# KV sums copied by ScalarE, norms rounded by GpSimd, and projected halves taken ahead of features

## The chip, the cores and the metric

The kernel runs on one core of a Trainium2 chip. The metric is the device time in microseconds of one execution. The engines are named as the profile names them: PE (TensorE), ACT (ScalarE), DVE (VectorE), POOL (GpSimd) and SP (SyncE, which here issues most of the DMAs). Each engine works through its own instruction queue in order, and waits on semaphores for the others.

## The reference

A batch of 8 sequences, 1024 tokens of 512 channels each, float32, goes through linear attention with random features, a layer norm, a matmul with a ternary weight, and a second layer norm. Cut to what matters:

```python
def feature_map(x, orf):                       # 16 heads of 32 channels, 128 features
    proj = x @ orf.T / d_k ** 0.25
    norm = jnp.sum(x * x, axis=-1, keepdims=True) / (2.0 * math.sqrt(d_k))
    return (jnp.exp(proj - norm) + EPS) / math.sqrt(m)

q = feature_map(split(x @ Wq.T + bq), orf)
k = feature_map(split(x @ Wk.T + bk), orf)
v = split(x @ Wv.T + bv)
kv = jnp.einsum('nlm,nld->nmd', k, v)
ksum = jnp.sum(k, axis=1)
out = jnp.einsum('nlm,nmd->nld', q, concatenate([kv, ksum[..., None]], axis=-1))
out = (out[..., :-1] / out[..., -1:]) @ Wo.T + bo
x = layernorm(x + out)
x = layernorm(x + x @ (ternary(weight) * scale).T)
```

## The kernel before, in words

Float32 products are made of rounded parts: every operand is split into a high part (rounded by ACT) and a low part (the rest, by DVE or POOL), and a product is hi·hi + hi·lo + lo·hi.

The heads go in four groups of four (`g`), and each group is two units: an even unit `u = 2g` for the keys and an odd unit `u = 2g + 1` for the queries. A batch is units 0 to 7 and then the output stages. The order of everything is one list of stages, `SCHEDULE`, written by hand in `unit_stages` (lines 72 to 146) and `output_stages`. Every engine walks through this same list and does its own part of each stage, so a stage that is moved in the list moves in the queue of every engine that has a part in it. There is no planner with costs.

While unit `u` is at work, unit `u + 2` is projected and prepared. The stages, with `h` for a half of 512 tokens:

- `P` (line 951, PE): six of the twelve matmuls that project a half; two `P` stages make a half in one PSUM bank. The banks 0 and 1 alternate, and `P` waits for `L` of the half that had the bank before.
- `S` (lines 649 and 651, ACT): the projected half is copied to `unit_hi` and squared to `squares`. `L` (816, DVE): `unit_lo`.
- `Q` (824, 828, DVE): squares transposed and summed. `N` (834 to 839, DVE): the unit's norms are transposed (`norms_turned`), rounded (837) and the rest taken (839) into `norm_rows`.
- `LIFT` (SP): twelve DMAs bring `unit_hi` and `unit_lo` into `stacks`. `NL` (570, POOL): two DMAs bring the norm rows there.
- `F` (964 for keys, 969 for queries, PE; 668, ACT): products with the random features, then the exponential into `features`. For keys DVE adds the eight feature tiles up (777 for the first two, 780), in the same stages `F`.
- `G` (982, PE; the eight of a group): kv sums of the keys. With the last one, products of `ones` with DVE's added features (991), then ACT's copies (673, 678, 680). `KVT` (999, 1000, PE): kv sums transposed; ACT makes two small products with EPS (685, 687); DVE copies the transposed sums from PSUM into `kv_ksum` (842).
- `GG` (1014, PE): numerators and denominators of a half of the queries, which waits for `kv_ksum`; DVE transposes and inverts denominators (850, 853, 855). `R` (865, 867, DVE): the division.
- `XT` (636, ACT; 809, DVE; 580, POOL): the next batch's input split into `x_hi` and `x_lo`, in unit 5. Its first projection, at the end of unit 5, waits for `x_lo` of tile 3.
- In the output stages, `A`, `O`, `LN`, `Y`, `YT`, `FF`, `ST`, and `V` of the next batch (937 to 939). `Q` and `N` of the next batch's unit 1 stand there, too. `V`, `O` and `FF` share banks 0 and 1 with `P`.
- In the last batch (`b + 1 == B`), unit 5 has an order of its own, in which `KVT` follows `S` of half 1, and unit 7 has stages `AG` and `OK` in place of the whole-row output stages.

In batch 0, DVE also makes the ternary weights (`WF`, 755 and 756) between the stages of units 1 to 4.

Of the kernel before, what the change touches and what calls it, by code (L numbers as in the profile page):

```python
# [44 lines left out]
P = 128  # L45
# [26 lines left out]
def unit_stages(b, u):  # L72
# [24 lines left out]
    if is_key(u):  # L97
        st = [[("ST", b - 1, t)] if u == 0 and b else [] for t in (TT - 2, TT - 1)]
        half = [("G", b, g, r) for r in range(split_at(b, g))]
        early = [("AG", b, 0, 0), ("AG", b, 1, 0)] if b + 1 == B and u + 2 == NU else []  # L100
        if u == 0:
            seq = f(0, 1) + p[1] + s0 + l0 + f(2, 3) + q0 + st[0] + p[2] + f(4, 5) + half + s1 + l1 + f(6, 7) + q1 + norm + lift
            seq += st[1] + p[3]
        else:
            seq = f(0, 1) + p[0] + f(2, 3) + p[1] + s0 + l0 + f(4, 5) + q0 + half + p[2] + early + f(6, 7) + s1 + l1 + q1 + norm + lift + p[3]
        if u == 0 and b == 0:
            seq += [("WA", 0, k) for k in range(KT)]
        if u == 2 and b == 0:
            seq += [("WF", 0, 1)]
        if u == 2 and 0 < b < B - 1:  # L110
            seq += [("LX", b + 1, t) for t in range(5)]
        return seq
    kv = [("G", b, g, r) for r in range(split_at(b, g), 8)]
    if u < NU - 1:
        seq = p[0] + f(0, 1)
        if u == 1 and b == 0:
# [4 lines left out]
        elif u < NU - 3:  # L121
            seq += kv + f(2, 3) + p[1] + [("KVT", b, g)] + s0 + l0 + f(4, 5) + p[2] + f(6, 7) + s1 + q0 + [("GG", b, g, 0)]
            seq += l1 + p[3] + [("R", b, g, 0), ("GG", b, g, 1)] + q1 + norm + lift
        else:
# [121 lines left out]
def attention_kernel(nc, x, xt, wq, wk, wv, wo, wff, bias, bo, orf, out):  # L246
# [5 lines left out]
    with ctx:  # L252
# [68 lines left out]
        a_exp, a_kc = Signal("features_ready", 8 * NU), Signal("kv_copied", 3 * NG)  # L321
        a_c = Signal("eps_sums_ready", 2 * NG)
        a_ahi = Signal("a_hi_ready", TT)
        a_y, a_yhi, a_out = Signal("y_ready", TT), Signal("y_hi_ready", TT), Signal("out_ready", TT)

        v_xlo, v_plo, v_n = Signal("x_lo_ready", 4, 4), Signal("unit_lo_ready", 2 * NU), Signal("norms_ready", 3 * NU, 2)
        v_sq, v_ns = Signal("squares_read", 2 * NU, 2), Signal("squares_summed", 2 * NU, 2)
        v_ks = Signal("features_added", 7 * NG)
        v_kvc = Signal("kv_ready", NG)
        v_dt, v_dr = Signal("den_turned", 2 * NG, 1), Signal("den_steps", 2 * 2 * NG)  # L330
# [3 lines left out]

        g_xlo = Signal("x_lo_ready_pool", 4)
        g_xb = Signal("x_plus_bias_ready", TT)
        a_ghi, v_glo = Signal("group_hi_ready", 0), Signal("group_lo_ready", 0)
# [185 lines left out]
        def _(pool):  # L523
# [37 lines left out]
            def lift_norms(b, u):  # L561

                slot = ST[:, u % 2, :].bitcast(F32)
                wait(t_f.sem, t_f.nth(b, 8 * (u - 1)))
                if u == 1:
                    wait(t_ff.sem, t_ff.nth(b, 0))
                wait(v_n.sem, v_n.nth(b, 3 * u + 3))
                for part in range(2):
# [4 lines left out]
            for kind, b, at, _, _ in steps():  # L573
# [8 lines left out]
                elif kind == "A":  # L582
                    pool.wait_ge(d_xr[t].sem, d_xr[t].nth(b, 1))
                    if b + 1 == B and t < 2:
                        pool.wait_ge(v_kvc.sem, v_kvc.nth(b, NG))
                    elif b + 1 == B and t < 4:
# [10 lines left out]
        def _(act):  # L597
# [21 lines left out]
            for kind, b, at, ps, _ in steps():  # L619
# [62 lines left out]
                elif kind == "KVT":  # L682
# [3 lines left out]
                                         scale=EPS).then_inc(a_c.sem, 1)  # L686
                    nc.scalar.activation(CC[:, 2 * u:2 * u + 1], RSUM[:, 2 * u:2 * u + 1], ACT.Copy, scale=EPS).then_inc(a_c.sem, 1)
                elif kind == "A" and b + 1 < B:
                    split_hi(b, u)
# [21 lines left out]
        def _(dve):  # L711
# [76 lines left out]
            for kind, b, at, ps, _ in steps():  # L788
# [30 lines left out]
                elif kind == "Q":  # L819
# [6 lines left out]
                    if h == 0:  # L826
                        dve.wait_ge(v_n.sem, v_n.nth(b, 3 * (u - 1) + 1))
                    nc.vector.reduce_sum(NSUM[:, 16 * h:16 * (h + 1)], TQ[:, :].rearrange("p (a c) -> p a c", c=DH),
                                         axis=mybir.AxisListType.X).then_inc(v_ns.sem, 1)
                elif kind == "N":  # L830
                    n = 3 * u
                    dve.wait_ge(v_ns.sem, v_ns.nth(b, 2 * u + 2))
                    dve.wait_ge(v_n.sem, v_n.nth(b, n))
                    nc.vector.transpose(NT[:, :], NSUM).then_inc(v_n.sem, 1)
                    dve.wait_ge(v_n.sem, v_n.nth(b, n + 1))
                    norms_lifted(dve, b, u - 2)
                    nc.vector.tensor_copy(NN[:, u % 2, 0, :], NT[:, :]).then_inc(v_n.sem, 1)
                    dve.wait_ge(v_n.sem, v_n.nth(b, n + 2))
                    nc.vector.tensor_tensor(NN[:, u % 2, 1, :], NT[:, :], NN[:, u % 2, 0, :].bitcast(F32), ALU.subtract).then_inc(v_n.sem, 1)  # L839
                elif kind == "KVT":  # L840
                    dve.wait_ge(t_kvt.sem, t_kvt.nth(b, u + 1))
                    nc.vector.tensor_copy(KVS[:, u % 2, :], DN[:, 0:2 * P]).then_inc(v_kvc.sem, 1)
                elif kind == "F" and is_key(u) and not sums_on_pe(b, u // 2):
# [58 lines left out]
        def _(pe):  # L902
# [14 lines left out]
            for kind, b, at, ps, old in steps():  # L917
# [83 lines left out]
                elif kind == "GG":  # L1001
                    g, half = u, at[1]
                    if half == 0:

                        pe.wait_ge(v_kvc.sem, v_kvc.nth(b, g + 1))
                    else:
# [78 lines left out]
```

## Time and profile before

| what | value |
| --- | --- |
| median of 3 runs | 1294.76 us (1294.49 to 1295.84) |
| profiled execution, its own time | 1293.62 us |
| its span, first to last instruction | 1291.8 us |
| granted TensorE clock, mean | 0.999 |
| PE busy | 1262.5 us, 98% |
| DVE busy | 940.8 us, 73% |
| ACT busy | 700.6 us, 54% |
| POOL busy | 326.6 us, 25% |

The table's busy times are shares of the span, and an engine that isn't the bottleneck may be idle at no cost. Matmuls are pipelined: a matmul of 512 columns is shown with 0.39 us, but in an undisturbed row of them each starts 0.228 us after the one before. So a wait of PE is read best from the distance of two starts, against the same distance where nothing waits; the idle column of the trace shows somewhat less than that. Likewise ACT and DVE start an instruction some 0.1 us before the one ahead has ended.

### The profile page before, as it was taken

How to read it: one execution, taken by the hardware profiler on the slowest of the kernel's cores; microseconds unless marked ns; L12 is line 12 of the kernel's file. 1: busy time of each engine (PE TensorE's matmuls, PEld its weight loads, DVE VectorE, ACT ScalarE, POOL GpSimd, SP SyncE). 2: the span in 40 equal slices, each digit the busy share in tenths (PEclk: the TensorE clock that was granted, in tenths of full speed). 3: DMA queues.
4: the chain of work that ended last, by engine and by line, in shares of the span. 5: the costliest groups of instructions: out<-in, count | busy, mean ns of one | idle time of the engine just before them, and what ended most of it. 6: DMA issues, size and time to landing. Idle time of an engine off the chain costs nothing.

```text
span 1291.8 us, 24909 instructions
## 1 busy us (share of the span) xinstructions
PE 1262.5 (98%) x8626; PEld 958.8 (74%) x8626; DVE 940.8 (73%) x1775; ACT 700.6 (54%) x1403; POOL 326.6 (25%) x617
## 2 busy tenths in 40 slices
PE   9999999999999999999999999999999999999986
PEld 8767788677877678776787768876788767886665
DVE  6588765887658875788757886588865787657766
ACT  5557435574356743567336663367534665446534
POOL 0102342024310243103431034211252022420043
PEclk9999999999999999999999999999999999999999
DMA  6658404783146821567215762258612685036611
GB/s 236 153 125 220 100 33 121 171 195 88 52 110 174 201 61 58 129 171 187 62 58 130 181 169 65 65 132 209 153 44 71 152 208 142 33 87 144 149 58 65
DMA packets 82749, 160.33 MB, mean 124 GB/s; under 512 B 17856, under 2 KB 36416, under 8 KB 82112
## 3 DMA queue, kind: packets, MB, share of 16 engines
q1 hardware_dynamic: 68880, 139.78, 43.4%
q10 hardware_dynamic: 9648, 16.85, 3.4%
q0 software_dynamic: 4096, 2.11, 0.7%
q8 instruction: 69, 1.13, 0.4%
q14 instruction: 56, 0.46, 0.1%
HBM read 39.13 MB, written 16.78 MB: 43 GB/s over the span
## 4 chain that ended last, share of the span: by engine, by line
PE 76%; DVE 10%; issue 5%; ACT 4%; POOL 0%; ACTq 0%; DVEq 0%; POOLq 0%
PE ps L951 21%; PE ps L914 18%; PE ps L1014 7%; PE ps L964 6%; PE ps L982 5%; PE ps L937 4%; PE ps L939 4%; PE ps L938 4%; PE ps L969 4%; PE ps L1040 2%; ACT features L668 1%; DVE squares_turned L824 1%; DVE den L865 1%; DVE unit_lo L816 1%; DVE dens_turned L850 1%
## 5 line engine op out<-in xcount | busy, mean ns | idle before, releaser
L668 ACT ACTIVATE features<-ps 128x512 f32<-128x512 f32 x512 | 278.7, 604 | 248.2 <-PE ps L964 168.8
L570 POOL DMA_DIRECT2D stacks<-norm_rows x128 | 69.5, 546 | 530.4 <-DVE norm_rows L839 256.8
L964 PEld LDWEIGHTS ps<-orf_stack,stacks 98*128 98x128 f32 x1024 | 130.9, 192 | 28.0 <-issue 20.3
L914 PE MATMUL ps<-Wo_hi,stacks 128*128 128x512 f32 x448 | 150.5, 402 | 0.0
L641 ACT ACTIVATE values_then_attention<-ps 128x512 f32<-128x512 f32 x64 | 38.2, 597 | 196.9 <-PE ps L939 193.8
L780 DVE TENSOR_TENSOR den<-den,features 128x512 f32<-128x512 f32 x186 | 128.1, 689 | 12.9
L964 PE MATMUL ps<-orf_stack,stacks 98*128 98x128 f32 x1024 | 130.5, 272 | 0.0
L1014 PE MATMUL ps<-features,kv_ksum 128*32 128x512 f32 x1024 | 123.1, 598 | 3.3 <-ACT features L668 2.1
L816 DVE SCALAR_TENSOR_TENSOR unit_lo<-ps,cols,unit_hi 128x512 fp32r<-128x512 f32 x128 | 94.3, 736 | 39.0 <-ACT squares L651 39.0
L550 POOL TENSOR_SCALAR stats<-stats 128x1 f32<-128x1 f32 x128 | 36.0, 282 | 334.9 <-DVE stats L767 334.8
L914 PE MATMUL ps<-W_ternary,stacks 128*128 128x512 f32 x448 | 110.7, 389 | 0.0
L951 PE MATMUL ps<-x_hi,Wq_hi 128*128 128x512 f32 x256 | 103.5, 404 | 6.5 <-DVE unit_lo L816 6.5
L951 PE MATMUL ps<-x_hi,Wk_hi 128*128 128x512 f32 x256 | 108.5, 424 | 1.3 <-DVE x_lo L809 1.3
L937 PE MATMUL ps<-Wv_hi,x_hi 128*128 128x512 f32 x256 | 102.6, 401 | 0.8
L616 ACT ACTIVATE rows<-rows,stats 128x512 f32<-128x512 f32 x112 | 88.3, 815 | 26.4 <-POOL stats L554 25.6
L914 PEld LDWEIGHTS ps<-Wo_hi,stacks 128*128 128x128 f32 x448 | 84.2, 188 | 24.3 <-issue 7.1
L951 PE MATMUL ps<-x_lo,Wq_hi 128*128 128x512 f32 x256 | 101.1, 395 | 0.0
L951 PE MATMUL ps<-x_lo,Wk_hi 128*128 128x512 f32 x256 | 100.8, 394 | 0.0
L951 PE MATMUL ps<-x_hi,Wq_lo 128*128 128x512 f32 x256 | 100.6, 393 | 0.0
L951 PE MATMUL ps<-x_hi,Wk_lo 128*128 128x512 f32 x256 | 100.2, 391 | 0.0
L939 PE MATMUL ps<-Wv_hi,x_lo 128*128 128x512 f32 x256 | 100.0, 391 | 0.0
L938 PE MATMUL ps<-Wv_lo,x_hi 128*128 128x512 f32 x256 | 100.0, 390 | 0.0
(132 smaller groups left out, 2528.0 us busy)
## 6 DMA issues: line engine op xcount, KB each, us to landing
stacks<-unit_hi SPq DMA_DIRECT2D x512, 128.0 KB, 2.4
stacks<-unit_lo SPq DMA_DIRECT2D x256, 128.0 KB, 2.8
out<-rows ACTq DMA_DIRECT2D x56, 256.0 KB, 2.0
rows<-in_x_t SPq DMA_DIRECT2D x49, 256.0 KB, 3.4
rows<-in_x SPq DMA_DIRECT2D x32, 256.0 KB, 3.8
features<-in_x SPq DMA_DIRECT2D x32, 256.0 KB, 4.1
values_then_attention<-in_x_t SPq DMA_DIRECT2D x8, 256.0 KB, 7.4
stacks<-norm_rows POOLq DMA_DIRECT2D x128, 16.0 KB, 2.7
```

What stands on the lines that cost most here:

```text
L570: pool.dma_start(slot[row:row + 1, :].rearrange("o (t c) -> o t c", c=DH), NN[:, u % 2, part, :].bitcast(F32)).then_inc(n_lifted[u % 2].se ...
L616: nc.scalar.activation(row, row, ACT.Identity, scale=ln(k, t, 10), bias=ln(k, t, 11))\
L668: nc.scalar.activation(FE[:, n % 8, :, 0:M], ps[:, :].rearrange("p (a m) -> p a m", a=HG), ACT.Exp, scale=C_EXP).then_inc(a_exp.sem, 1)
L780: ins = nc.vector.tensor_tensor(total, total, FE[:, r, :, 0:M], ALU.add)
L816: nc.vector.scalar_tensor_tensor(out=EL[:, u % 2, half], in0=ps[:, :], scalar=BC[:, u:u + 1], in1=EH[:, u % 2, half].bitcast(F32), op0=ALU ...
L914: last = mm(out, a, b, start=(n == 0), stop=(n == len(terms) - 1))
L937: mm(ps[:, :], XH[:, k, c], WH["v"][:, k, :], start=(k == 0), stop=False)
L938: mm(ps[:, :], XH[:, k, c], WL["v"][:, k, :], start=False, stop=False)
L939: last = mm(ps[:, :], XL[:, k, c], WH["v"][:, k, :], start=False, stop=(k == KT - 1))
L951: last = mm(ps[:, :], *terms[n], start=(n == 0), stop=(n == len(terms) - 1))
L964: last = mm(ps[:, M * h:M * (h + 1)], slot[0:QK, L * h + P * r:L * h + P * (r + 1)], ORF[0:QK, h, :], start=True, stop=True)
L1014: last = mm(bank[DH * h:DH * (h + 1), :], KVS[:, g % 2, c + DH * h:c + DH * (h + 1)], FE[:, HG * half + h, :, 0:M], start=True, stop=True, ...
```

## The change

Four things:

1. The copy of the transposed kv sums (stage `KVT`) goes from DVE to ACT, behind ACT's two small products. Who waited for DVE's signal (PE in `GG`, POOL in `A` of the last batch) waits for ACT's.
2. In `N`, DVE only transposes the norms. POOL rounds them and takes the rest, at the beginning of its stage `NL`, and issues the two DMAs as before. DVE's next transposition waits for POOL's reading of the last one.
3. In even units other than 0, `S` and `L` stand right behind the `P` that ends their half, ahead of `F` (with its exponentials and additions); `Q` of half 0 stands behind the next `P`.
4. In units 1 and 3 the same: `S` and `L` of half 0 are the second thing in the unit, ahead of `F(0, 1)` and `G`; `S` and `L` of half 1 stand ahead of `F(6, 7)`; `Q` of half 0 takes their old place behind `KVT`. At the unit's end, `Q` of half 1 goes ahead of `GG` of half 1, and both divisions `R` go to the end. Units 0, 5 and 7 keep their order.

```diff
-            seq = f(0, 1) + p[0] + f(2, 3) + p[1] + s0 + l0 + f(4, 5) + q0 + half + p[2] + early + f(6, 7) + s1 + l1 + q1 + norm + lift + p[3]
+            seq = f(0, 1) + p[0] + s0 + l0 + f(2, 3) + p[1] + q0 + f(4, 5) + half + p[2] + early + s1 + l1 + f(6, 7) + q1 + norm + lift + p[3]
...
-        seq = p[0] + f(0, 1)
+        seq = p[0] + (s0 + l0 if u < NU - 3 else []) + f(0, 1)
...
-            seq += kv + f(2, 3) + p[1] + [("KVT", b, g)] + s0 + l0 + f(4, 5) + p[2] + f(6, 7) + s1 + q0 + [("GG", b, g, 0)]
-            seq += l1 + p[3] + [("R", b, g, 0), ("GG", b, g, 1)] + q1 + norm + lift
+            seq += kv + f(2, 3) + p[1] + [("KVT", b, g)] + q0 + f(4, 5) + p[2] + s1 + l1 + f(6, 7) + [("GG", b, g, 0)]
+            seq += p[3] + q1 + [("GG", b, g, 1)] + norm + lift + [("R", b, g, 0)]
...
             def lift_norms(b, u):
                 slot = ST[:, u % 2, :].bitcast(F32)
+                pool.wait_ge(v_n.sem, v_n.nth(b, u + 1))
+                norms_lifted(pool, b, u - 2)
+                nc.gpsimd.tensor_copy(NN[:, u % 2, 0, :], NT[:, :]).then_inc(g_n.sem, 1)
+                pool.wait_ge(g_n.sem, g_n.nth(b, 2 * u + 1))
+                nc.gpsimd.tensor_tensor(NN[:, u % 2, 1, :], NT[:, :], NN[:, u % 2, 0, :].bitcast(F32), ALU.subtract)\
+                    .then_inc(g_n.sem, 1)
                 wait(t_f.sem, t_f.nth(b, 8 * (u - 1)))
                 if u == 1:
                     wait(t_ff.sem, t_ff.nth(b, 0))
-                wait(v_n.sem, v_n.nth(b, 3 * u + 3))
+                wait(g_n.sem, g_n.nth(b, 2 * u + 2))
...
+                    act.wait_ge(t_kvt.sem, t_kvt.nth(b, u + 1))
+                    nc.scalar.activation(KVS[:, u % 2, :], DN[:, 0:2 * P], ACT.Copy).then_inc(a_kv.sem, 1)
...
                 elif kind == "N":
-                    n = 3 * u
                     dve.wait_ge(v_ns.sem, v_ns.nth(b, 2 * u + 2))
-                    dve.wait_ge(v_n.sem, v_n.nth(b, n))
+                    if b or u:
+                        dve.wait_ge(g_n.sem, g_n.nth(b, 2 * u))
                     nc.vector.transpose(NT[:, :], NSUM).then_inc(v_n.sem, 1)
-                    dve.wait_ge(v_n.sem, v_n.nth(b, n + 1))
-                    norms_lifted(dve, b, u - 2)
-                    nc.vector.tensor_copy(NN[:, u % 2, 0, :], NT[:, :]).then_inc(v_n.sem, 1)
-                    dve.wait_ge(v_n.sem, v_n.nth(b, n + 2))
-                    nc.vector.tensor_tensor(NN[:, u % 2, 1, :], NT[:, :], NN[:, u % 2, 0, :].bitcast(F32), ALU.subtract).then_inc(v_n.sem, 1)
-                elif kind == "KVT":
-                    dve.wait_ge(t_kvt.sem, t_kvt.nth(b, u + 1))
-                    nc.vector.tensor_copy(KVS[:, u % 2, :], DN[:, 0:2 * P]).then_inc(v_kvc.sem, 1)
...
-                        pe.wait_ge(v_kvc.sem, v_kvc.nth(b, g + 1))
+                        pe.wait_ge(a_kv.sem, a_kv.nth(b, g + 1))
```

## Rows read from the trace of the kernel before

**Rows 1.** The page's part 1: busy time, share and instructions.

```profile
PE 1262.5 (98%) x8626; PEld 958.8 (74%) x8626; DVE 940.8 (73%) x1775; ACT 700.6 (54%) x1403; POOL 326.6 (25%) x617
```

**Rows 2.** PE's waits, whole span: us, times, longest.

```profile
PE ps L951 <- DVE unit_lo L816: 6.5, 10, 1.3
...
PE ps L951 <- DVE x_lo L809: 1.3, 7, 0.2
```

**Rows 3.** PE's timeline, batch 2: start, us, instruction, idle before.

```profile
394.39 1.01 PE L964 MATMUL ps<-orf_stack,stacks 98*128 98x128 f32 x8
395.24 0.46 PE L951 MATMUL ps<-x_hi,Wq_hi 128*128 128x512 f32 x1
...
441.55 1.01 PE L964 MATMUL ps<-orf_stack,stacks 98*128 98x128 f32 x8
443.03 0.50 PE L951 MATMUL ps<-x_hi,Wq_hi 128*128 128x512 f32 x1 [0.47 <-DVE unit_lo L816]
...
448.24 0.40 PE L991 MATMUL ps<-den,ones 128*32 128x128 f32 x8
```

**Rows 4.** DVE's timeline, unit 6 of batch 2.

```profile
438.24 0.18 DVE L837 CAST norm_rows<-norms_turned 128x32 fp32r<-128x32 f32 x1
...
440.04 0.68 DVE L777 TENSOR_TENSOR den<-features 128x512 f32<-128x512 f32 x1
...
442.23 0.74 DVE L816 SCALAR_TENSOR_TENSOR unit_lo<-ps,cols,unit_hi 128x512 fp32r<-128x512 f32 x1
...
445.63 1.48 DVE L780 TENSOR_TENSOR den<-den,features 128x512 f32<-128x512 f32 x2
```

**Rows 5.** PE's timeline, batches 0 and 7.

```profile
79.90 0.50 PE L951 MATMUL ps<-x_hi,Wq_hi 128*128 128x512 f32 x1 [0.99 <-DVE unit_lo L816]
...
1208.43 0.50 PE L951 MATMUL ps<-x_hi,Wq_hi 128*128 128x512 f32 x1 [1.33 <-DVE unit_lo L816]
```

**Rows 6.** Timelines, PE and DVE, output stages.

```profile
492.08 1.98 PE L914 MATMUL ps<-W_ternary,stacks 128*128 128x512 f32 x8
494.17 0.50 PE L937 MATMUL ps<-Wv_hi,x_hi 128*128 128x512 f32 x1
...
493.43 0.69 DVE L886 TENSOR_TENSOR rows<-ps,features 128x512 f32<-128x512 f32 x1
```

**Rows 7.** Timelines, unit 5 of batch 2.

```profile
426.08 0.22 ACT L687 ACTIVATE cols<-cols 128x1 f32<-128x1 f32 x1
426.18 0.70 ACT L649 ACTIVATE unit_hi<-ps,cols 128x512 fp32r<-128x512 f32 x1
...
426.32 0.43 DVE L842 COPY kv_ksum<-ps 128x256 f32<-128x256 f32 x1 [0.57 <-PE ps L1000]
...
430.02 0.69 DVE L809 TENSOR_TENSOR x_lo<-rows,x_hi 128x512 fp32r<-128x512 f32 x1 [0.57 <-ACT x_hi L636]
...
430.86 0.47 PE L951 MATMUL ps<-x_hi,Wk_hi 128*128 128x512 f32 x1 [0.19 <-DVE x_lo L809]
```

**Rows 8.** ACT's forms: count, busy us, mean ns.

```profile
L641 ACT ACTIVATE values_then_attention<-ps 128x512 f32<-128x512 f32 x64 | 38.2, 597 | 196.9 <-PE ps L939 193.8 <-DVE stacks L785 3.1
...
L680 ACT ACTIVATE kv_ksum_t<-ps,cols 128x128 f32<-128x128 f32 x32 | 11.5, 359 | 0.0
```

**Rows 9.** Timelines, unit 5 of batch 7.

```profile
1216.81 0.25 ACT L687 ACTIVATE cols<-cols 128x1 f32<-128x1 f32 x1
...
1215.71 1.92 PE L1014 MATMUL ps<-features,kv_ksum 128*32 128x512 f32 x16
```

**Rows 10.** GpSimd: additions, timeline, the page's norm DMAs.

```profile
L590 POOL TENSOR_TENSOR rows<-rows,out_bias 128x512 f32<-128x512 f32 x32 | 41.3, 1306 | 10.9 <-DVE kv_ksum L842 10.8
...
439.23 1.09 POOL L570 DMA_DIRECT2D stacks<-norm_rows  x2 [2.21 <-DVE norm_rows L839]
...
stacks<-norm_rows POOLq DMA_DIRECT2D x128, 16.0 KB, 2.7
```

**Rows 11.** Line 785: count, ns least, median, most.

```profile
L785 DVE TENSOR_TENSOR stacks<-values_then_attention,stacks x56: 656/684/922, 144.1 to 1127.2; 128x512 fp32r<-128x512 f32 x56
```

More of the change, by code:

```diff
@@ L322, in attention_kernel @@
         a_c = Signal("eps_sums_ready", 2 * NG)
+        a_kv = Signal("kv_ready", NG)
         a_ahi = Signal("a_hi_ready", TT)
         a_y, a_yhi, a_out = Signal("y_ready", TT), Signal("y_hi_ready", TT), Signal("out_ready", TT)
-        v_xlo, v_plo, v_n = Signal("x_lo_ready", 4, 4), Signal("unit_lo_ready", 2 * NU), Signal("norms_ready", 3 * NU, 2)
+        v_xlo, v_plo, v_n = Signal("x_lo_ready", 4, 4), Signal("unit_lo_ready", 2 * NU), Signal("norms_turned", NU, 1)
         v_sq, v_ns = Signal("squares_read", 2 * NU, 2), Signal("squares_summed", 2 * NU, 2)
         v_ks = Signal("features_added", 7 * NG)
-        v_kvc = Signal("kv_ready", NG)
         v_dt, v_dr = Signal("den_turned", 2 * NG, 1), Signal("den_steps", 2 * 2 * NG)
@@ L335, in attention_kernel @@
         g_xlo = Signal("x_lo_ready_pool", 4)
+        g_n = Signal("norms_ready", 2 * NU)
         g_xb = Signal("x_plus_bias_ready", TT)
@@ L584, in _ @@
                     if b + 1 == B and t < 2:
-                        pool.wait_ge(v_kvc.sem, v_kvc.nth(b, NG))
+                        pool.wait_ge(a_kv.sem, a_kv.nth(b, NG))
                     elif b + 1 == B and t < 4:
@@ L826, in _ @@
                     if h == 0:
-                        dve.wait_ge(v_n.sem, v_n.nth(b, 3 * (u - 1) + 1))
+                        dve.wait_ge(v_n.sem, v_n.nth(b, u))
                     nc.vector.reduce_sum(NSUM[:, 16 * h:16 * (h + 1)], TQ[:, :].rearrange("p (a c) -> p a c", c=DH),
```

## The prediction

> **What bounds the kernel.** I read the page's busy times first, then the table of waits of PE, then the timelines around each wait. PE has work for 1262.5 of 1291.8 us [rows 1]: only what PE waits for, or waits for newly, can move the time. Its waits name few releasers, and two of them touch this change [rows 2]: the first matmul of a projected half waits for DVE's `unit_lo` of an older half (10 times), and the first product of the next batch for `x_lo` (7 times; a wait of GG for ACT's features follows it closely). A batch is 157.1 us long and repeats, so the second is one place in batches 0 to 6, and so are seven of the ten.
>
> **The wait on unit_lo, unit 6 (it goes).** In an undisturbed even unit PE starts the next half 395.24 - 394.39 = 0.85 us after its last pair of feature tiles; in unit 6 it takes 443.03 - 441.55 = 1.48 [rows 3]. The 0.63 is that L (`unit_lo` of half 0) ran on DVE only at 442.23 to 442.97 [rows 4], behind three feature additions. Its input was projected five us earlier. After the change ACT takes the half right behind its matmuls and L stands behind one addition. A late start also delays the second weight load by about 0.05. Is L then early enough? The additions start at 440.04. DVE loses the two norm operations in front (438.24, its twin at 438.45, 0.47 with their gaps), but gets 0.45 later through unit 5 (below): 440.0 again. An addition takes 0.6 to 0.8, so L ends at 441.5, against 442.4 + 0.45 where PE wants it. The wait goes: 0.65 x 7 = **4.55 us gained**.
>
> **What is late next.** The last addition must be done before PE's `ones` product at 448.24 [rows 3]; it ended at 447.11 (445.63 + 1.48). Now L of half 1 stands ahead of the last two additions: +0.66, less 0.18 of gaps between neighbouring additions that L fills. It ends at 447.6; PE arrives at 448.24 + 0.45 - 0.65 = 448.04. Cover 0.46 us, in unit 7. Units 3 and 5 are built alike, but PE comes no 0.65 earlier there, and the backlog is about 0.3 smaller: behind GG(1) the division R(0) (1.5 us) is new, while Q(1) (1.4) and the two norm operations (0.4) are gone. The cover is some 0.8 to 1.0.
>
> **The same wait elsewhere.** In batch 0, unit 2 waits 0.99 by the idle column [rows 5], and unit 4 shows one more like it. The idle column of unit 6 shows 0.47 for 0.63, so these are some 1.17 each, plus 0.05. DVE also turns the ternary weights there and its backlog moves only by the same 0.3, so the `ones` product meets the last addition 0.3 us early: net 0.92 each, **1.85 gained**. In batch 7, unit 5 waits 1.33 idle, 1.48 by starts, for `unit_lo` of half 1 [rows 5]; L(1) is now ahead of two additions of 0.7 to 0.8. **1.45 gained.**
>
> **The norm turned in the output stage.** V follows eight ternary products: 492.08 + 8 x 0.228 = 493.90, but starts at 494.17 since DVE's row addition ended at 494.12 [rows 6]. Cast and subtraction of the norms stand just before, in a chain of DVE without a gap. They go to GpSimd: DVE is 0.45 earlier, V starts on time. 0.27 x 7 = **1.9 gained**.
>
> **ACT's copy, unit 5 (it costs).** Unit 5 keeps its order. ACT works without a gap there, from the KV copies to the last `x_hi`; the turned sums are ready at 426.3, when DVE's copy began and when ACT's two small EPS products ended (426.08 + 0.22); S started at 426.18, overlapping them [rows 7]. A copy of 128x256 on ACT is not in the trace. The nearest rows are 359 ns for 128x128 and 597 ns for 128x512, from PSUM to SBUF [rows 8]: 0.44 by interpolation, of which the next instruction overlaps about 0.12. S starts at 426.32 + 0.32 = 426.64: 0.45 late. Bounds: below 0.25 (the copy hides partly in the overlap), above 0.72 (0.14 of waiting and the 0.58 pitch of ACT's 0.70 us half-tile operations). I take 0.45, next to both forms. All ACT work behind it slides, among it `x_hi` of tile 3, whose `x_lo` releases PE at 430.86 [rows 7]. DVE stood idle for 0.57 before that `x_lo` [rows 7], so it can't make it up. The features wait that follows slides with it and isn't paid twice. 0.45 x 7 = **3.15 lost**.
>
> **ACT's copy elsewhere.** In units 1 and 3 S no longer follows it and PE has a projection half before GG: covered, at 0.45 if not. In unit 7 GG(0) waits for the copy; the 0.44 and DVE's 0.42 [rows 7] are alike and both start behind the same transposes: 0.05 x 7 = **0.35 lost** (0 to 0.15 each). In batch 7, unit 5, the copy stands behind S(1) in ACT's queue: it can begin only at 1217.04 and end at 1217.46, where GG(0) had started at 1215.71 behind DVE's copy [rows 9]. GG(1) waits for GG(0)'s turned denominators, so all slides: **1.75 lost**. In the last unit 7 it puts two features tiles and two rounded groups 0.3 later, on the way to GG's attention: **0.3 lost** (0 to 0.45).
>
> **GpSimd's two operations.** 128x32 is not in its trace; its 128x512 addition takes 1.3 us [rows 10] and bounds each from above; nothing excludes 0.2, DVE's time, as the lower bound. I take 0.35, so the rows are ready 0.4 later than by DVE, or 2.3 at the upper bound. In unit 5 the lift was issued at 439.23 for 1.09 us and lands 2.7 later, at 443.0 [rows 10]; unit 7's features start 12 products of 0.23 behind 443.03, at 445.8. 2.8 us of cover: nothing, and up to 0 at both bounds. The copies stand in GpSimd's queue where it only waited to issue the lift; the next things queued there are `x_lo` tiles and layer scales, reached later. Without that cover each us would cost a us per unit.
>
> The Trainium skill, GPSIMD Engine Reference, Engine selection, speaks against the move: two-input elementwise work is some 2x slower there than on the Vector engine, one-input work about equal. The trace agrees in the ratio (1.31 against 0.69 us for 128x512). By it the pair costs an estimated 0.18 + 0.39 us in place of my 0.70, and the sum stays.
>
> The moved stages issue nothing new; lifts of SP are freed up to 1.4 us earlier since S(1) and L(1) precede the last features, and SP's queue holds nothing that this overtakes.
>
> **Sum.** Gained 4.55 + 1.85 + 1.45 + 1.9 = 9.75; lost 3.15 + 0.35 + 1.75 + 0.3 = 5.55; net 4.2 us. The profiled execution took 1293.62 us (span 1291.8), so 1289.4; the median of the runs is 1.14 higher: 1294.76 - 4.2 = **1290.6 us**.
>
> **Rivals.** (A) *No measurable change*: ACT's copy costs its upper bound, 0.72, in unit 5 (+1.9 us) and the output-stage wait merely passes to another operation there (half of 1.9 back): 1293.4 us. For it: ACT has no gap and the wait on PE's transposes is new in its queue. Against: the row of 128x128 is half of that length. (B) *Slower*: the feature additions become the bound. L(1) now stands before the last two, and L(1) waits for ACT's S(1). If the last addition comes d later than I count, the `ones` products wait d - 0.46 in unit 7 and d - 0.8 or more in units 3 and 5. It cancels the gain at d = 0.95 and is slower by over 0.2% from 1.05; at 1.2 it costs 0.74 + 0.4 + 0.3 = 1.44 a batch, some 11 in all: 1301 us. For it: DVE works without a gap through unit 6. Against: S(1) ends 1.6 us before DVE comes to L(1). (C) *More gained*: the copy costs 0.25 in unit 5 (1.4 back), batch 0 gives nothing back (0.6), and the batch-7 copy is hidden in half (0.9): 1287.7 us. (D) The change doesn't do what it says, as ACT's S waits for the slot to be lifted: excluded, since PE's features of the same slot wait for the same landings.
>
> DVE's subtraction of two SBUF operands (L785) takes 684 ns at the median and 922 at most [rows 11]; the longest lie beside GpSimd's long additions. The Trainium skill, VectorE: DVE Perf Modes, "Two Vector instructions with no wait between them", says that an instruction's second SBUF operand is read through an interface shared with GpSimd. If GpSimd's new subtraction fell on an addition, the 0.24 of the row would go into d of rival B; it falls beside R, which reads one SBUF tile, so it only supports B a little.
>
> **Chances.** Forecast 0.58 (own range 1288.3 to 1292.9), A 0.20, B 0.10, C 0.12. Two runs of this kernel can be told apart from about 0.2%, 2.6 us. Faster by more: 0.85 of the forecast's and C: 0.61. Within: the rest of the forecast's 0.09 and 0.17 of A: 0.26. Slower: B and the 0.03 of A in which something is added to it: 0.13. Range 1287.0 to 1296.5: it holds C, A and the mild end of B.
>
> **What would show it.** PE's waits on `unit_lo` gone from unit 6 and batch 0, none on DVE's `den` in their place; `x_lo` waits up from 0.36 to 0.8 each by starts; V's start 0.27 earlier; an ACT copy of 0.38 to 0.44 us; GG(0) of batch 7, unit 5 waiting for it by 1.75; DVE 37 us less busy (32 x 0.42 of copies, 64 x 0.37 of norm operations). Waits of PE on `den`, or on landings of norm rows, would prove me wrong.

## The result, and the profile after

The median is 1286.05 us (4 runs, 1285.8 to 1289.02), against 1294.72 us of the kernel before in the same session (1294.49 to 1295.84): ratio 0.9937 [0.9925 to 0.9949]. The profiled execution took 1285.8 us, span 1284.0, against 1293.62 and 1291.8. The forecast was 1290.6 (1287.0 to 1296.5): the sign is right, the time lies below the range. The gain is 8.7 us on the medians and 7.8 on the two profiled executions; forecast were 4.2.

The page's busy times of the kernel after, to be set beside [rows 1]. DVE has 42.5 us less (37 were forecast; the three groups that left it are 37.5 by themselves), ACT 12.9 more and POOL 36.9 more; PE, which sets the time, has the same matmuls.

```profile
PE 1258.4 (98%) x8626; PEld 957.5 (75%) x8626; DVE 898.3 (70%) x1615; ACT 713.5 (56%) x1435; POOL 363.5 (28%) x745
```

PE's waits of the kernel after, whole span (us in total, times, longest), to be set beside [rows 2]:

```profile
PE ps L952 <- DVE x_lo L818: 4.2, 7, 0.6
...
PE ps L1015 <- ACT kv_ksum L696: 1.6, 1, 1.6
```

No wait of PE on `unit_lo` is left (before: 6.5 us, 10 times), and none on DVE's `den` has come. Waits on `x_lo` grew from 1.3 to 4.2 us, and batch 7 has its new wait of 1.6 on ACT's copy. These are the waits that the prediction named. A second execution of the same kernel has one more, on a landing of norm rows (e12, below).

PE in unit 6 of batch 2 (start, us, instruction), to be set beside [rows 3]:

```profile
438.10 1.01 PE L965 MATMUL ps<-orf_stack,stacks 98*128 98x128 f32 x8
438.94 0.45 PE L952 MATMUL ps<-x_hi,Wq_hi 128*128 128x512 f32 x1
...
444.10 0.40 PE L992 MATMUL ps<-den,ones 128*32 128x128 f32 x8
```

The half starts 0.84 us after the feature tiles (1.48 before). DVE in the same unit, to be set beside [rows 4]:

```profile
436.11 0.68 DVE L786 TENSOR_TENSOR den<-features 128x512 f32<-128x512 f32 x1
436.71 0.74 DVE L825 SCALAR_TENSOR_TENSOR unit_lo<-ps,cols,unit_hi 128x512 fp32r<-128x512 f32 x1
...
441.51 0.74 DVE L825 SCALAR_TENSOR_TENSOR unit_lo<-ps,cols,unit_hi 128x512 fp32r<-128x512 f32 x1
442.17 1.48 DVE L789 TENSOR_TENSOR den<-den,features 128x512 f32<-128x512 f32 x2
```

`L` of half 0 stands behind one addition and ends at 437.45, 1.5 us ahead of PE. The last addition ends at 442.17 + 1.48 = 443.65, 0.45 before PE's product at 444.10; the forecast was 0.46.

The output stage, PE and then DVE, to be set beside [rows 6]. V starts 7 x 0.228 us behind the first row, on time, and DVE's row addition ends at 489.47, 0.26 before V starts:

```profile
488.14 1.75 PE L915 MATMUL ps<-W_ternary,stacks 128*128 128x512 f32 x7
489.73 0.39 PE L938 MATMUL ps<-Wv_hi,x_hi 128*128 128x512 f32 x1
```

```profile
488.79 0.68 DVE L887 TENSOR_TENSOR rows<-ps,features 128x512 f32<-128x512 f32 x1
```

Unit 5 of batch 2, to be set beside [rows 7]: ACT, then PE. ACT's copy takes 0.39 us and `S` follows 0.28 behind its start; PE's first projection of the next batch waits 0.60 by the idle column (0.19 before).

```profile
422.22 0.22 ACT L694 ACTIVATE cols<-cols 128x1 f32<-128x1 f32 x1
422.45 0.39 ACT L696 ACTIVATE kv_ksum<-ps 128x256 f32<-128x256 f32 x1
422.73 0.68 ACT L656 ACTIVATE unit_hi<-ps,cols 128x512 fp32r<-128x512 f32 x1
```

```profile
427.40 0.47 PE L952 MATMUL ps<-x_hi,Wk_hi 128*128 128x512 f32 x1 [0.60 <-DVE x_lo L818]
```

That place lies at 430.86 before [rows 7] and at 427.40 now; the same place a batch later is at 587.89 and 583.76. This batch is 156.36 us long instead of 157.03.

The groups of the new operations (line, form, count, busy us, mean ns), ACT's and then GpSimd's, to be set beside [rows 8, 10]:

```profile
L696 ACT ACTIVATE kv_ksum<-ps 128x256 f32<-128x256 f32 x32 | 12.4, 387 | 0.5
```

```profile
L569 POOL TENSOR_TENSOR norm_rows<-norms_turned,norm_rows 128x32 fp32r<-128x32 f32 x64 | 18.8, 294 | 5.4
L567 POOL CAST norm_rows<-norms_turned 128x32 fp32r<-128x32 f32 x64 | 16.5, 257 | 443.4 <-DVE norms_turned L843 443.4
```

Batch 7, unit 5, ACT and PE, to be set beside [rows 9]: the copy starts at 1207.95, and PE starts `GG` 0.49 later, after 1.62 us of waiting.

```profile
1207.95 0.43 ACT L696 ACTIVATE kv_ksum<-ps 128x256 f32<-128x256 f32 x1
```

```profile
1208.44 1.92 PE L1015 MATMUL ps<-features,kv_ksum 128*32 128x512 f32 x16 [1.62 <-ACT kv_ksum L696]
```

**Where the time came from.** The two kernels issue the same 8626 matmuls in the same order, so start can be set against start, one by one. The steps in the difference, us:

| place | forecast | measured |
| --- | --- | --- |
| wait on `unit_lo`, unit 6, x7 | -4.55 | 7 x -(0.63 + 0.06) = -4.8 |
| the same in batch 0, units 2 and 4 | -1.85 | -2.31 |
| the same in batch 7, unit 5 | -1.45 | -1.58 |
| V in the output stage, x7 | -1.9 | 7 x -(0.27 + 0.11) = -2.64 |
| `x_lo` of tile 3, x7 | +3.15 | 7 x 0.41 = +2.88 |
| `GG(0)` in unit 7, x7 | +0.35 | 7 x -0.044 = -0.31 |
| `GG(0)` in batch 7, unit 5 | +1.75 | +1.69 |
| batch 7 behind it | +0.3 | -0.55 |
| PE's first 24 matmuls (products of `ones` with itself) | 0 | -0.29 |
| sum | -4.2 | -7.9 |

Where two numbers stand in brackets, the first is the wait itself, the second the later start of the matmul after it. The spans differ by 7.8.

### The profile page after: what moved, and what is told of

Read it like the earlier page. It is cut to its first block, busy times and chain, and to the rows that moved or that the text cites. A ratio compares the mean times of both kernels' runs of the same rounds, so it can differ in the third digit from the quotient of the medians.

```text
span 1284.0 us, 24908 instructions
## 1 busy us (share of the span) xinstructions
PE 1258.4 (98%) x8626; PEld 957.5 (75%) x8626; DVE 898.3 (70%) x1615; ACT 713.5 (56%) x1435; POOL 363.5 (28%) x745
## 4 chain that ended last, share of the span: by engine, by line
PE 86%; ACT 5%; issue 2%; DVE 2%; POOL 0%; ACTq 0%; POOLq 0%; DVEq 0%
PE ps L952 25%; PE ps L915 21%; PE ps L965 9%; PE ps L1015 8%; PE ps L983 5%; PE ps L970 4%; PE ps L938 4%; PE ps L940 4%; PE ps L939 4%; PE ps L1041 2%; ACT features L675 2%; ACT squares L658 1%; ACT x_hi L643 1%; PE ps L992 1%; DVE stats L773 0%
## 5 line engine op out<-in xcount | busy, mean ns | idle before, releaser
L567 POOL CAST norm_rows<-norms_turned 128x32 fp32r<-128x32 f32 x64 | 16.5, 257 | 443.4 <-DVE norms_turned L843 443.4
L656 ACT ACTIVATE unit_hi<-ps,cols 128x512 fp32r<-128x512 f32 x128 | 88.4, 690 | 65.6 <-PE ps L952 65.6
```

Of the source, the lines that this page charges most:

```text
L656: nc.scalar.activation(EH[:, u % 2, half], ps[:, :], ACT.Identity, bias=BC[:, u:u + 1]).then_inc(a_p.sem, 1)
```

## Experiments

Ratios are to the kernel before, with 95% intervals. "Start against start" compares the matmuls of two profiled executions as in the table. "Cover" is the time by which something is ready before PE needs it.

**One part at a time.** The kernel before with one of the three parts each.

e1, the norms alone (the edit in words):

```diff
+ GpSimd, at the head of NL: norm_rows[0] = cast(norms_turned); norm_rows[1] = norms_turned - norm_rows[0]
- VectorE, in N: the same two operations
```

> Only the rounding of the turned norms moves to GpSimd; the copy stays on DVE and the order is the old one. My theory (each wait of PE on DVE shrinks by what is taken out of DVE's gapless chain ahead of it, up to its own length): the norm operations are 0.47 us of chain, so V's wait goes (0.38 us with the late weight load, 7 times: 2.6), the unit_lo wait of unit 6 shrinks by 0.47 (7 times: 3.3), those of batch 0 by about 0.4 each and that of batch 7 by 0.4: 7.2 us faster in all, about 1287.5 us. Rival (the order is what removes the unit_lo waits): only V gains, 2.6 us, about 1292 us.

Measured: 1289.82 us (1287.96 to 1290.31), ratio 0.996 [0.9945 to 0.9975]. Start against start, unit 6 gains 0.45 to 0.53 in each batch, V gains 0.27 + 0.10 in each, batch 0 gains 1.05 in two steps, batch 7's unit 5 0.54. So the norms leaving DVE give all of V's gain, and most of unit 6's by themselves: there the two operations stood in the queue ahead of `L`. Near the end, unit 7's first features of the last batch lost 0.83 against the kernel before. Their lift's last landing was at 1221.92 and they started at 1222.01. Against PE's work the last `unit_lo` row was issued 0.43 later, and it took 4.40 us to land instead of 4.00. Behind this wait the granted clock fell (mean 0.93 from 1216 to 1240), 1.4 us, and PE's first 24 matmuls took 0.78 longer; without these the time stands near the first expectation.

e2, the order alone:

```diff
- f(0,1) + p[0] + f(2,3) + p[1] + s0 + l0 + f(4,5) + q0 + half + p[2] + early + f(6,7) + s1 + l1 + q1
+ f(0,1) + p[0] + s0 + l0 + f(2,3) + p[1] + q0 + f(4,5) + half + p[2] + early + s1 + l1 + f(6,7) + q1
```

(and units 1 and 3 as in the change.)

> Only the order of the stages; copy and norms stay on DVE. My theory: all unit_lo waits go as in the changed kernel (0.69 x 7 + 2.4 in batch 0 + 1.6 in batch 7 = 8.8 us), V's wait stays, and DVE, not relieved of the norms, now ends its last feature addition 0.1 to 0.2 us after PE wants it in unit 7 (1 us in all): 7.5 to 8.5 us faster, about 1286.5 us. Rival (the relief of DVE is what makes the order work): waits of PE on den in all odd units, and less than 4 us gained.

Measured: 1287.57 us (1287.08 to 1292.2), ratio 0.9951 [0.9935 to 0.9967]. Unit 6 gains 0.60 to 0.64 each, V nothing. Batch 0 gains 1.16 and 1.18 but gives back 0.54 and 0.58 (products with `ones` that wait for DVE's last addition) and 0.45 (`GG`, which waits for DVE's copy). In the kernel after, the two at the `ones` products are 0.07 each and the one at `GG` is gone. That one waited for the copy itself, which ACT now makes. The other two have both the norms and the copies taken out of DVE's queue ahead of them; no run has the new order and the norms on GpSimd with the copy on DVE, so how much each pays isn't shown. The gains of e1 and e2 in unit 6 are the same wait and don't add.

e3, the copy alone:

```diff
-                elif kind == "KVT":                                   # VectorE
-                    nc.vector.tensor_copy(KVS[:, u % 2, :], DN[:, 0:2 * P]).then_inc(v_kvc.sem, 1)
+                    nc.scalar.activation(KVS[:, u % 2, :], DN[:, 0:2 * P], ACT.Copy).then_inc(a_kv.sem, 1)
```

> Only the copy of the turned kv sums moves to ACT; norms on DVE, old order. My theory: the x_lo wait grows by 0.41 us (7 times: 2.9), GG(0) of batch 7, unit 5 waits 1.7, the copy leaves DVE in stretches where it is idle anyway: 4 to 4.6 us slower, about 1299 us. Rival (DVE's wait for the transposes at the head of its queue was worth something): no slower than before, 1293 to 1295 us.

Measured: 1303.24 us (1303.09 to 1303.37), ratio 1.0066 [1.0051 to 1.0081]: 8.0 us over the 1295.2 of its session, where 4 to 4.6 were expected. The `x_lo` place lost 0.41 each and batch 7 1.69, as counted. But in units 1 and 3 of every batch the last features and `GG` also came 0.19 + 0.10 late (0.35 + 0.10 in two of the sixteen; about 0.3 x 16 = 4.8). Under the old order `S` stands behind the copy there.

**Is the order in units 1 and 3 what hides the copy?** e7: the kernel after, with the old order in units 1 and 3. e8: the same with the old order in units 2, 4 and 6.

```diff
- seq = p[0] + (s0 + l0 if u < NU - 3 else []) + f(0, 1)    # e7: units 1 and 3
+ seq = p[0] + f(0, 1)
...                                                         # and the rest of these units as before
```

> The changed kernel with the old order in units 1 and 3; even units as changed. My theory (ACT's copy costs nothing in units 1 and 3 only because S and L were moved out from behind it): PE waits 0.2 + 0.1 us before features 6 and 7 in each of these units, 0.3 x 16 = 4.8 us slower than the changed kernel, about 0.9975 of the kernel before. Rival (the odd order matters for DVE's backlog at the start of the even unit alone, which is 0.3 us): no more than 1 us slower than the changed kernel.

> The changed kernel with the old order in units 2, 4 and 6; units 1 and 3 as changed. My theory: the unit_lo wait of unit 6 comes back with 0.63 less the 0.47 of DVE's chain freed by the norms (0.2 us with the late weight load, 7 times: 1.1 to 1.4), in batch 0 0.4 to 0.5 in each of two units, in batch 7 0.7 to 1.0: 3 us slower than the changed kernel, about 0.996 of the kernel before. Rival (the order alone removes the wait): 8 us slower.

Measured: e7 1293.27 us (1291.26 to 1296.89, 10 runs), ratio 0.9993 [0.9983 to 1.0003]; e8 1292.79 (1290.58 to 1293.28, 9 runs), 0.9977 [0.9967 to 0.9987]. In e7 the 0.19 and 0.10 of e3 are back in both units of all batches, and no wait on `unit_lo` comes: the new order there does nothing for `unit_lo`, it is the cover of ACT's copy, worth some 5 us. (e7's profiled execution is 6.2 us longer than that of the kernel after, its ratio 0.0056 higher, which is 7.2 us; what lies beyond these 5 us has no one place.) In e8 unit 6 waits only 0.14 to 0.17 + 0.06, once 0.49, batch 0 0.64 and 0.68, and batch 7's unit 5 1.00 + 0.10; 2.8 us of its loss are PE at a lower granted clock behind the wait in batch 7 (below).

**The copy in unit 5.** e4: the kernel after, DVE copies in unit 5 of all batches, where ACT has no gap. e5: the same but for the last batch.

```diff
+                    if u != 2:        # e5: if u != 2 or b + 1 == B; u is the group, 2 that of unit 5
                     nc.scalar.activation(KVS[:, u % 2, :], DN[:, 0:2 * P], ACT.Copy).then_inc(a_kv.sem, 1)
...
+                elif kind == "KVT" and u == 2:                        # VectorE; e5: and b + 1 < B
+                    nc.vector.tensor_copy(KVS[:, u % 2, :], DN[:, 0:2 * P]).then_inc(a_kv.sem, 1)
```

> The changed kernel, but in group 2 (unit 5, all batches) the copy is DVE's again, the other groups' stay on ACT. My theory: the x_lo wait falls back from 0.77 to 0.36 us (7 times: 2.9 gained) and GG(0) of batch 7 starts 1.7 earlier: 4 to 4.6 us faster than the changed kernel, about 1281.7 us, and no wait elsewhere grows. Rival (unit 5's ACT chain sets the end of the unit, so that another wait of the same size shows behind it, or DVE's chain comes later): 0 to 2 us faster than the changed kernel.

> The changed kernel, but in unit 5 of batches 0 to 6 the copy is DVE's; in the last batch it stays on ACT. My theory after the run with all of group 2 on DVE (there the last batch ran into the landing of unit 7's lift, waited 1.63 us and PE then ran at its lower clock for a microsecond and more): this one avoids that and keeps 0.405 x 7 = 2.8 us against the changed kernel, about 0.9910 of the kernel before. Rival (the missing gain of that run was spread, not in the last batch): no better than it, 0.993.

Measured: e4 1285.39 us (1284.37 to 1286.81), ratio 0.993 [0.9914 to 0.9947]; e5 1284.45 (1283.7 to 1287.06), 0.9921 [0.9906 to 0.9936]. Start against start with the kernel after, both give back 0.40 to 0.41 at six of the `x_lo` places and 0.37 in batch 0: 2.8 us, the whole term. (The intervals overlap with the kernel after's, 0.9925 to 0.9949; the medians alone don't tell them apart.) In e4 `GG(0)` of batch 7 also comes 1.68 earlier, and 1.63 of that is lost 12 us later. With 1.4 at a low clock behind it and 1.0 more at PE's first 24 matmuls, e4's execution is 0.8 shorter than that of the kernel after, where 4 to 4.6 were expected. PE's timeline of e4:

```profile
1217.70 0.93 PE L974 MATMUL ps<-stacks,orf_stack 98*128 98x512 f32 x3 [1.47 <-ACT features L675]
```

The trace puts the wait to ACT's features, which had long been done. The four `unit_lo` rows of this lift, issued at 1211.3 to 1213.1, took 2.3, 3.5 in the middle and 4.5 us at most to land; the last landed at 1217.61, 0.09 before PE started. The times from issue to landing (least, median, most) of these four in e4, and in the kernel after:

```profile
DMA to landing us min/median/max: 2.3/3.5/4.5
```

```profile
DMA to landing us min/median/max: 2.3/2.4/2.7
```

In e4 (and in the kernel before, where the last landing was at 1227.28 and PE started at 1227.37) GpSimd's norm rows go out among them; in the kernel after they go out behind them. The kernel before, e1, e2, e4, e6 and e11 all have PE's start 0.09 behind the last landing of this lift, though in all but e6 the trace names another releaser or none. That the norm rows are what delays the last row isn't shown: no run moves them alone.

**The lift that lands late.** e6: as e4, and the last batch's four `unit_lo` rows issued by GpSimd at once. e11: as e4, and PE sums two parts of unit 6 ahead of these features.

```diff
-                        sp.dma_start(slot[DH:2 * DH, ...], lo[...])      # e6, last batch, unit 7
+                        pool.dma_start(slot[DH:2 * DH, ...], lo[...])
...
-        seq = [...] + f(0, 1, 2) + kv + ...                              # e11, last batch, unit 7
+        seq = [...] + kv[0:2] + f(0, 1, 2) + kv[2:] + ...
```

> All of group 2's copies on DVE as before, and in the last batch the four unit_lo DMAs of unit 7's lift are issued by GpSimd, beside SP's eight, on a semaphore of their own. My theory (PE's first features of unit 7 waited for the last landing of that lift, though the profile puts the wait down to ACT): they land some 2.5 us earlier, the wait of 1.63 us and the low clock behind it go, 2.8 + 1.7 = 4.5 us faster than the changed kernel, about 0.990 of the kernel before. Rival (the wait is for ACT's features, as the profile has it): PE waits at the same place as long as in the run with the copy alone, 0.993.

> The kernel after, with VectorE copying the turned sums of unit 5 (as in e4_copy_dve_in_unit5) and, in the last batch, TensorE summing two of the eight parts of unit 6 (0.98 us) ahead of the first features of unit 7 instead of behind them. In e4 these features waited 1.47 us for the last landing of unit_lo rows at 1217.61, while nothing else was ready in TensorE's order. If that landing is the bound there, the wait falls to 0.5 us and 0.98 us is gained on e4: 1284.4 us. Rival: the features are then late for ScalarE and the later products wait for it: 1285.4 us, as e4.

Measured: e6 1284.29 us (1281.92 to 1285.87), ratio 0.9915 [0.99 to 0.993]; e11 1283.83 (1281.84 to 1284.04), 0.9911 [0.9897 to 0.9925]. In e6 the wait hardly shrank (1.47 to 1.27), and now it is the `unit_hi` rows that land last:

```profile
1217.29 0.93 PE L987 MATMUL ps<-stacks,orf_stack 98*128 98x512 f32 x3 [1.27 <-DMA stacks<-unit_hi]
```

The rows of the lift issued from two queues hardly land sooner: SP's took up to 5.7 us, and the last landed at 1217.20, 0.4 before e4's. The Trainium skill, DMA: Bandwidth & Descriptors, Issuing engines are not separate DMA queues, says that DMAs started by different engines run on the same 16 DMA engines; the trace agrees. e11 leaves the transfers alone and gives PE other work. The last row lands at 1218.40, and PE, which has summed in the meantime, waits 0.45 for it:

```profile
1218.49 0.94 PE L974 MATMUL ps<-stacks,orf_stack 98*128 98x512 f32 x3 [0.45 <-issue]
```

The median of e11 is the lowest here, though its interval overlaps with e6's and e5's; beside the unchanged kernel after on the same chip (e12, 1288.72) it is 4.9 us faster. Its profiled execution lost 1.8 us in batch 0, unit 6, at and behind a wait on norm rows (below).

**Are the two margins real?** e9: one spare reduction on DVE ahead of unit 6's last addition, in batches 0 to 6. e10: eight spare casts on GpSimd ahead of the norms' rounding.

```diff
+                    if r == 7 and g + 1 == NG:                                             # e9
+                        nc.vector.reduce_sum(SPARE[:, 0, 0:HG], FE[:, r, :, 0:M], axis=mybir.AxisListType.X)
...
+                for k in range(8):                                                         # e10
+                    nc.gpsimd.tensor_copy(SPARE[:, k, :], NT[:, :])
```

> The kernel after, with one spare reduction of 128x512 on VectorE (about 0.69 us, its result is read by nobody) right ahead of the last addition of unit 6, in batches 0 to 6. The prediction priced the margin of the last addition: in the kernel after the last addition ends 0.41 us before the product with ones (L992) starts. If the additions still wait for nothing but VectorE's own queue, the product with ones starts 0.69 - 0.41 = 0.28 us late in each of 7 batches, 2.0 us in all: 1288.0 us. Rival: the queue has slack behind the additions' inputs (VectorE waits for ScalarE there), and the reduction is hidden: 1286.0 us, no product with ones late.

> The kernel after, with 8 spare casts of 128x32 on GpSimd (about 0.257 us each, 2.05 us in all, read by nobody) ahead of the rounding of the norms in every unit. The landings of the norm rows had 1.62 us (unit 7), 1.1 us (unit 1) and, in batch 0, 0.72 us (unit 7) before the features that need them. If that is the cover of GpSimd's rounding, the features of unit 1 start 0.95 us and those of unit 7 0.43 us late in each of 7 batches and 1.3 us in batch 0, about 10 to 11 us in all: 1296 to 1297 us. Rival: unit_hi and unit_lo rows are what lands last anyway, and only batch 0 and the last batch feel it: 1288 us.

Measured: e9 1288.46 us (1287.13 to 1289.57), ratio 0.995 [0.9936 to 0.9963]; e10 1305.16 (1304.33 to 1308.28), 1.0077 [1.0062 to 1.0092]. Medians can't tell e9 from e12, but start against start the product with `ones` is 0.19 to 0.20 late in all seven batches, 1.4 us in all. DVE and PE of e9 show it: the addition ends at 444.64 and releases PE at 444.69.

```profile
443.36 0.69 DVE L791 TENSOR_REDUCE spare<-features 128x4 f32<-128x512 f32 x1
443.96 0.68 DVE L792 TENSOR_TENSOR den<-den,features 128x512 f32<-128x512 f32 x1
```

```profile
444.69 0.43 PE L995 MATMUL ps<-den,ones 128*32 128x128 f32 x8
```

So rival B's mechanism is real, with some 0.40 us of margin: 0.60 more on DVE cost 0.20. In e10 PE waits for the norm rows 13 times:

```profile
PE ps L973 <- DMA stacks<-norm_rows: 15.0, 13, 2.1
```

Unit 1 lost 1.21 to 1.32 in batches 1 to 7 (1.14 of cover, 2.24 us of casts), unit 7 between 0.14 and 2.26. In unit 7 the casts took 1.26 us (in batch 0 1.74), which its cover would nearly hide, but the second norm row took 3.5 to 5.8 us from issue to landing, and the losses vary with it. With a share of low clock at the end that is 16.4 us over e12, and 10 to 11 were expected. GpSimd's longer way costs nothing in the first profile of the change because the cover is there, but the prediction had looked at one unit 7 only, that of batch 2: 2.7 us there before, 1.8 to 3.0 in the others, 2.0 in unit 1 and 1.24 in batch 0's unit 7. In the kernel after it is 1.62 us in batch 2's unit 7, 1.06 to 1.51 in the others, 1.14 in unit 1 on average and 0.72 in batch 0's unit 7.

**The spread of the kernel after.** e12 is the kernel after, unchanged.

> The kernel after once more, unchanged, for its spread and as the neighbour of the three others on this chip: 1286.05 us by its earlier median. If the 0.9 us by which the medians gained more than the profiled executions is the spread of single executions, a new profile and a new median differ from the old ones by up to 1 us; if it is part of the change, profile and median stand as before, 1285.8 and 1286.05.

Measured: 1288.72 us (1286.9 to 1289.98, 5 runs), ratio 0.9951 [0.9939 to 0.9964], span 1288.2: 4.2 us longer than the first profile, start against start in two places. The first is PE in batch 0, unit 7:

```profile
130.25 0.71 PE L970 MATMUL ps<-stacks,orf_stack 98*128 98x512 f32 x2 [0.87 <-DMA stacks<-norm_rows]
```

The norm row issued at 123.98 landed at 130.12, after 6.1 us (4.5 in the first profile, where PE came 0.72 after the landing). Four 256-KB loads of the next rows were issued by SP beside it, in the kernel before as well: there the row took 4.9 us, with 1.24 of cover left. e5 shows the same wait at the same place (+0.95), and e11 has one in batch 0's unit 6 (0.63), where the row took 8.0 us. So of the ten profiled executions with the norms on GpSimd (e10 left out) three wait for norm rows, of the three with the norms on DVE none. The second is behind the wait in batch 7, in PE's rows of e12:

```profile
1209.73 2.91 PE L1015 MATMUL ps<-features,kv_ksum 128*32 128x512 f32 x16 [1.62 <-ACT kv_ksum L696]
1213.51 3.64 PE L1015 MATMUL ps<-features,kv_ksum 128*32 128x512 f32 x16 [0.87 <-issue]
```

Sixteen products take 2.9 and 3.6 us where they took 1.92. The granted clock of this stretch, in e12 and in the kernel after (window, its length, busy us of PE, PEld, DVE, ACT, POOL, granted clock, DMA share, GB/s):

```profile
1209.00:1215.00 6.00, 4.40 (x24) 0.96 (x28) 2.95 (x6) 1.66 (x6) 0.00 (x0) 0.63 0.78 178
```

```profile
1209.00:1215.00 6.00, 5.12 (x49) 2.55 (x41) 4.33 (x10) 1.56 (x4) 1.06 (x4) 1.00 0.90 204
```

Before it, PE had waited 1.62 us in both. So this wait costs 1.7 us in one execution, and in another 2.8 more, by a stretch that is in part at 1.2 instead of 2.4 GHz. The same happened in e8 (2.8) and e10 (1.6) behind the same wait, and in e1, e4 and e6 behind a wait of 1.3 to 1.5 us on the lift. In the kernel after, e3, e5, e7 and e9 no matmul slowed behind the same 1.6 us, so the wait doesn't make it certain.

## Why the prediction was wrong

The mechanism was right: each wait that the prediction said would go is gone, and the two that it said would come in unit 5 have come, at their places. Two small losses that it named in unit 7 came out as gains (below). "The wait on unit_lo, unit 6", "the `x_lo` place" and "batch 7, unit 5" are within 0.3 us of what was measured. What failed is the size of four terms, all with the same sign. They are 2.7 of the 3.7 us by which the sum was short; 0.3 more are PE's first 24 matmuls, which the change doesn't touch, and 0.7 are small differences in the other four terms:

- **The norm turned in the output stage**, "0.27 x 7 = 1.9 gained". It is 0.377 x 7 = 2.64. For unit 6 I had counted that a late start also delays the second weight load; it does so at V too, by 0.106 (0.27 + 0.106 = 0.377). I left it out there. e1 shows both steps.
- **"In batch 0 ... the `ones` product meets the last addition 0.3 us early"**: it met it 0.07 early; 0.46 us more gained. I had moved DVE's backlog by too little: in e2, with the norms and the copy still on DVE, the paybacks are 0.54 and 0.58. Which of the two operations' leaving makes up the difference stays open.
- **"In unit 7 GG(0) waits for the copy ... 0.35 lost"**: 0.31 gained. ACT's copy takes 387 ns against DVE's 425; I had interpolated 0.44 between [rows 8], where the time is nearer to the 359. The step is 0.04 in e3, with the copy alone, and 0 in e1 and e2, with the copy on DVE.
- **"In the last unit 7 ... 0.3 lost"**: 0.55 gained. In the kernel before, unit 7's first features waited there for the last landing of their lift (1227.28, PE at 1227.37). The waits put that to ACT's features, so I didn't see that a transfer bound, and not the work that I shifted. Whatever brings PE there later, or the lift earlier, takes this wait away; e3 shows the same 0.84 gained with nothing of the other parts, and e4 the opposite. The 0.55 is a balance: 0.84 here and 0.33 and 0.28 at two waits on ACT beside it, less 0.47 in the next three products and 0.43 further on, whose cause isn't known.

The remaining 0.9 us are the step from profile to median: I added the 1.14 by which the median of before lay above its profile. After, the median lay 0.25 above. The second measurement of the kernel after (1288.72, e12) shows that this is no property of the change: single executions differ by 1.0 us at the norm rows of batch 0 and by 2.8 at the clock behind batch 7's wait. The first is a step of the prediction that failed in part: "2.8 us of cover: nothing" was read at one place, and waits on landings of norm rows were its own sign of being wrong. The e12 session alone would give a gain of 6.4 us.

Of the rivals, C (1287.7) came nearest, with one of its three reasons: batch 0 gave back nearly nothing, but the copy in unit 5 cost 0.41, not 0.25, and in batch 7 nothing of it was hidden. B did not happen, but e9 puts its threshold where the prediction did. A is refuted by the 0.41. One "covered" was right: in units 1 and 3 the copy is hidden only by the new order (e3, e7), as the prediction said, at 0.3 and not 0.45 without it.

## What to carry to other kernels

Price a wait by the distance of two starts on the bound engine, second weight load included, at every place and not only at the first. Where the trace names a releaser that had long been done, look up when the transfers for that matmul landed: a lift 0.09 us ahead of PE is the bound, and then work moved around it is worth nothing or double. A queue's two operations of 0.2 us are worth moving only away from an engine that stands ahead of a wait; and a part that loses 8.0 us by itself (the copy) may lose half of that behind a new order (2.88 + 1.69 in unit 5, nothing in units 1 and 3). Read a margin at every place that it stands for: the least of them decides.

## What the runs showed of the hardware

- GpSimd's cast and subtraction of 128x32 take 0.21 and 0.25 us, but 0.58 to 0.63 when they start behind a DVE instruction with two operands from SBUF that is under way (7 of 64 casts, beside `x_lo`; 7 of 64 subtractions, beside feature additions; one subtraction in batch 0 took 0.75). Seven casts that started 0.07 us ahead of such an addition kept their 0.21. POOL and DVE of the kernel after:

```profile
365.60 0.59 POOL L569 TENSOR_TENSOR norm_rows<-norms_turned,norm_rows 128x32 fp32r<-128x32 f32 x1
...
445.60 0.25 POOL L569 TENSOR_TENSOR norm_rows<-norms_turned,norm_rows 128x32 fp32r<-128x32 f32 x1
```

```profile
365.39 1.49 DVE L789 TENSOR_TENSOR den<-den,features 128x512 f32<-128x512 f32 x2
```

  DVE's own additions kept their 0.69. Eight casts in a row took 1.26 us in unit 7 and 2.24 in unit 1, beside two such additions (e10). The Trainium skill, SBUF — State Buffer, SBUF: two separate sides, says that GpSimd and such a DVE instruction take the shared ports in turn, each for a whole instruction; the trace agrees: this subtraction starts 0.2 us behind the first of the two additions and ends 0.12 behind its end.
- A late start of PE costs more than its delay: the weight load behind it, and the matmul that needs it, come 0.05 to 0.11 us late as well, at each of the 17 places (unit 6, V, batches 0 and 7) where a wait went.
- PE's first 24 matmuls (48 rows of the trace, from 1.4 us on) step 0.21 us apart and later 0.11, and the change comes at different times, though the kernels don't differ there: e4 ends them 1.4 us behind e5 and 1.2 behind e11, e12 0.2 behind the first profile of the same kernel.
- Two 16-KB transfers of GpSimd's take 2.7 us to land as a rule (page of the kernel before, [rows 10]), and the second of them 4.5 or 6.1 beside four 256-KB loads, in two executions of one kernel.
